# Fourth attention: six multiplications into a free PSUM bank in each unit but a batch's last

## The chip, the cores and the metric

The kernel runs on one core of one Trainium2 chip. The metric is the device time of one execution in microseconds (us): the time before is the median of three runs, 3110.26 us (3109.85 to 3111.97).

## The reference, cut to what matters

The program is a chain of four transformer layers, each an attention-like block and a feed-forward block with a layer norm behind each. The change is in the attention of the fourth layer, for 8 sequences of 256 tokens with 256 channels. What it computes:

```python
q = _rope(x @ Wq)              # 16 heads, two halves of 16 each
k = _rope(x @ Wk)              # 4 key heads, two halves
energy = einsum('bqhad,bkhad->bahqk', q, k)       # a = the two halves
scores = softmax(mask(energy) / sqrt(D))
diff = scores[:, 0] - lam * scores[:, 1]
diff = softmax(mask(diff))
att = einsum('bhqv,bvhd->bqhd', diff, v)
att = att * rsqrt(mean(att * att) + EPS) * rms_w * (1 - LAM_INIT)
return att.reshape(b, s, E) @ Wo
```

So there are two softmaxes with a difference between them, then the product with the values, a norm over each head, and the output projection.

## The kernel before

`l3_attention` (line 1578) is written for five engines that run at the same time and meet only at semaphores. Each engine has its own instruction stream in a fixed order; an instruction waits for a semaphore and everything behind it on that engine waits too.

After the projections, the work goes over batches `b` (one sequence of 256 tokens, two tiles of 128) and, in each batch, over eight **units** `i` from 0 to 7. A unit is one quarter `r = i // 2` of the heads (four heads, one in each group of 32 rows) and one half `a = i % 2` of the head. TensorE's order in a unit is `sequence` (line 1779):

- `scores(b, i)` (line 1708): waits `p_exp`, that is until ScalarE has read the scores of the unit before out of PSUM banks 0 to 3 (there is one set of them), then 16 small multiplications (line 1721) and 8 that add the mask (line 1725); each half signals `s_ps`.
- in odd units `values(b, i)` (lines 1738 to 1752), the product of the turned probabilities with the values, into bank 6 (`OT`); in even units `turn_back` (line 1754), two transposes into bank 7 (`OB`).
- `turn(b, i)` (line 1727): six transposes of the probabilities of the unit three before into banks 4 and 5 (line 1736), when ScalarE has signalled `p_ready`.
- in unit 6 `turn_output` of the batch before (line 1767, into `OT`), in unit 7 `project_output` (line 1775, into `OB`).

VectorE's order in a unit is: `maxima` (line 1961, needs `s_ps`; ScalarE's exponentials need it), in even units half a `difference` (line 1979), `second_maxima` (lines 1989 and 1991), `out_of_psum` (line 1997: it copies what `turn` has put into bank 5), in odd units `values_out` (line 2002) and in even ones `take_output` (lines 2008 and 2009, which signals `on_raw`), and at the end of odd units `ratios` (line 1968 and on, needs `p_exp`) with another half of a `difference`. In unit 5 the norm of the batch before stands between (lines 2016 to 2022), in unit 7 the sum into `x_sb` and its statistics.

ScalarE's order in a unit is: the eight exponentials of the scores with their sums (line 1864), the copy out of bank 4 (line 1872), four exponentials of the second softmax (line 1881, signals `p_ready`). GpSimd adds the mask (line 1816), computes the other half of each difference (lines 1826 and 1829), and squares the output (line 1833).

Batch 0 runs as `opening`, batches 1 to 7 in a loop, and what is left over as `closing`. The waits, the order and the banks are written out by hand; nothing plans them.

Of the kernel before, what the change touches and what calls it, by code (L numbers as in the profile page):

```python
# [30 lines left out]
def bc(ap, axis, n):  # L31

    wide = ap.unsqueeze(axis)
    shape = list(wide.shape)
    shape[axis] = n
    return wide.broadcast_to(tuple(shape))
# [1541 lines left out]
def l3_attention(nc, c, x_sb, mv, xT, w, psum):  # L1578
# [4 lines left out]
    HD, G, R, A = 16, 4, 4, 2  # L1583
# [5 lines left out]
    with ExitStack() as ctx:  # L1589
# [35 lines left out]
        OT, OB = psum[:, 6, :], psum[:, 7, :]  # L1625
# [26 lines left out]
        on_raw = sem("on_raw")  # L1652
# [12 lines left out]
        def live(i, lag, opening, closing):  # L1665

            return i >= lag if opening else i < lag if closing else True
# [5 lines left out]
        with nc.Block() as block:  # L1673
# [14 lines left out]
            def _(pe):  # L1688
                mm = nc.tensor.matmul
# [20 lines left out]
                def scores(b, i, opening):  # L1710
                    r, a = i // A, i % A
                    if i == 0:
                        pe.wait_ge(k_staged, b + 1)
                    if a == 0:
                        pe.wait_ge(q_staged[r], b * 16 + 16)
                    if not (opening and i == 0):
                        pe.wait_ge(p_exp, b * NU + i)
                    for t in range(TT):
                        for g in range(G):
                            rows = slice(32 * g, 32 * g + 32)  # L1720
                            mm(S[:, g, t * P:t * P + (t + 1) * P], qr[rows, a, r, t * P:(t + 1) * P], kr[rows, a, 0:(t + 1) * P],  # L1721
                               start=(t == 0), stop=False, tile_position=(32 * g, 0))
                    for g in range(G):
                        for t in range(TT):
                            last = mm(S[:, g, 2 * t * P:(2 * t + 1) * P], c["idb"], c["maskb"], start=False, stop=(t == TT - 1))  # L1725
                        if g % 2 == 1:
                            last.then_inc(s_ps, 1)

                def turn(b, i):
                    s = b * NU + i - 3  # L1730
                    r, heads = (i - 3) // 2 % R, part(i - 3)
                    pe.wait_ge(p_ready, s + 1)
                    for j, copied in enumerate((pt_even, pt_odd)):
                        pe.wait_ge(copied, s + 1)
                        for k in range(3):
                            last = nc.tensor.transpose(PT[j][:, k * P:(k + 1) * P], pr[:, r, 1, heads.start + j, k * P:(k + 1) * P], c["id"])
                        last.then_inc(pt_ps, 1)

                def values(b, i):
                    q = b * R + (i - 5) // 2  # L1740
                    r = (i - 5) // 2 % R
                    pe.wait_ge(pt_even, 2 * q + 3)
                    pe.wait_ge(pt_odd, 2 * q + 3)
                    if r == 0:
                        pe.wait_ge(v_staged, b * 16 + 16)
                    for g in range(G):
                        cols = slice(32 * g, 32 * g + 32)
                        mm(OT[cols, 0:T], vs[:, 0, g, :], pt[:, r % 2, g, 0:T], start=True, stop=False, tile_position=(0, 32 * g))
                    for g in range(G):
                        cols = slice(32 * g, 32 * g + 32)  # L1750
                        last = mm(OT[cols, P:T], vs[:, 1, g, :], pt[:, r % 2, g, T:T + P], start=False, stop=True, tile_position=(0, 32 * g))
                    last.then_inc(av_ps, 1)

                def turn_back(b, i, first):
                    q = b * R + (i - 6) // 2
                    pe.wait_ge(ots_ready, q + 1)
                    if not first:
                        pe.wait_ge(on_raw, q)
                    for t in range(TT):
                        last = nc.tensor.transpose(OB[:, t * P:(t + 1) * P], ots[:, t * P:(t + 1) * P], c["id"])  # L1760
                    last.then_inc(back_ps, 1)

                def turn_output(b):
                    pe.wait_ge(on_ready, b + 1)
                    for h in range(KD):
                        for t in range(TT):
                            last = nc.tensor.transpose(OT[:, (h * TT + t) * P:(h * TT + t + 1) * P],
                                                       on[:, t, h * P:(h + 1) * P], c["id"])
                    last.then_inc(oT_ps, 1)

                def project_output(b):
                    pe.wait_ge(oT_ready, b + 1)
                    for t in range(TT):
                        for k in range(KD):
                            last = mm(OB[:, t * D:(t + 1) * D], oT[:, k, t * P:(t + 1) * P], wo[:, k, :],
                                      start=(k == 0), stop=(k == KD - 1))
                    last.then_inc(y_ps, 1)

                def sequence(b, opening=False, closing=False):
                    for i in range(NU):  # L1780
                        if not closing:
                            scores(b, i, opening)
                        if i % 2 == 1 and live(i, 5, opening, closing):
                            if i == 7 and not opening:
                                pe.wait_ge(oT_ready, b)
                            values(b, i)
                        if i % 2 == 0 and live(i, 6, opening, closing):
                            if i == 0:
                                pe.wait_ge(z_ready, b)
                            turn_back(b, i, opening)  # L1790
                        if live(i, 3, opening, closing):
                            turn(b, i)
                        if i == 6 and not opening:
                            turn_output(b - 1)
                        if i == 7 and not opening:
                            if not closing:
                                pe.wait_ge(on_raw, b * R + 1)
                            project_output(b - 1)
# [5 lines left out]
                pe.wait_ge(proj_out, NCH * NP)  # L1804
                pe.wait_ge(set_up, 6)
                sequence(0, opening=True)
                with pe.Fori(0, B - 1) as b:
                    sequence(b + 1)
                sequence(B, closing=True)

            @block.gpsimd
# [750 lines left out]
```

## Time and profile before

| | before |
|---|---|
| median of three runs | 3110.26 us |
| the profiled execution's own time | 3111.67 us |
| its span, first to last instruction | 3109.9 us |
| mean granted TensorE clock over the span | 0.917 |
| the fourth attention's units, first scores to last | 2115 to 2573 us |
| one batch in the loop | 58.0 us |

The page gives each engine's busy share of the whole span and, in 40 slices, its busy share and the granted TensorE clock in tenths. The fourth attention lies in slices 28 to 33. The clock has two levels, 1.2 GHz (0.5 in the rows) and 2.4 GHz (1.0); a mean between them over a stretch means that both occurred. Times in the timeline are from the start of the span. A row of the timeline merges instructions of one line that follow each other.

### The profile page before, as it was taken

To read this page: it belongs to the slowest core of one execution; us is meant where nothing else is said; L and a number is where in the kernel's file an instruction comes from. 1 tells how busy PE (TensorE), PEld (TensorE's weight loads), DVE (VectorE), ACT (ScalarE), POOL (GpSimd) and SP (SyncE) were. 2 spreads that over 40 slices of the span, in tenths; PEclk is the share of its full clock that TensorE was granted. 3 is DMA by queue.
4 is the path that set the end of the run, shared out by engine and by line. 5 is a ranking of instruction groups with operands and counts; after the bars stand their busy time and mean duration, and the time that the engine had idled before them with its cause. 6 is when DMAs were issued, how large, how long until landed. Compare 5 with 4: busy or idle time off the path is not lost. (4 is left out here: it accounts for less than half of the span.)

```text
span 3109.9 us, 43072 instructions
## 1 busy us (share of the span) xinstructions
PE 2608.6 (84%) x14256; PEld 1883.3 (61%) x14256; DVE 1858.5 (60%) x4295; ACT 1310.5 (42%) x3605; POOL 359.7 (12%) x392
## 2 busy tenths in 40 slices
PE   7988999889999999998698877796555654999997
PEld 5665544457776777677476665543443433877876
DVE  3665233445464555445645757546888886777777
ACT  4663455533443344334222132205777773332322
POOL 2440000000000000000121000003444440000000
PEclk9998999989999999999899888896777776999998
DMA  3002000000000000002000000100000003000000
GB/s 148 10 7 82 1 0 0 0 35 1 3 3 3 0 3 3 3 0 75 16 0 0 0 0 0 37 6 29 24 19 19 24 9 132 1 1 0 0 0 27
DMA packets 26415, 56.11 MB, mean 18 GB/s; under 512 B 3696, under 2 KB 22896, under 8 KB 24688
## 3 DMA queue, kind: packets, MB, share of 16 engines
q1 hardware_dynamic: 26352, 55.32, 4.8%
q8 instruction: 33, 0.54, 0.1%
q14 instruction: 30, 0.25, 0.0%
HBM read 39.59 MB, written 2.10 MB: 13 GB/s over the span
## 5 line engine op out<-in xcount | busy, mean ns | idle before, releaser
L1864 ACT ACTIVATE l3a_pr<-psum,l3a_nm 128x128 f32<-128x128 f32 (+1 forms) x512 | 207.1, 430 | 202.8 <-DVE l3a_nm L1961 202.8
L1721 PE MATMUL psum<-l3a_kr,l3a_qr 32*128 32x128 f32 (+1 forms) x1024 | 91.1, 491 | 180.3 <-ACT l3a_pr L1864 176.9
L108 DVE TENSOR_TENSOR x_sb<-psum,x_sb 128x512 f32 (+2 forms) x48 | 41.7, 868 | 235.2 <-PE psum L950 135.5
L757 DVE TENSOR_TENSOR l0f_hg<-l0f_sq,psum 128x512 f32<-128x512 f32 x128 | 87.8, 688 | 151.1 <-ACT l0f_sq L689 148.3
L1721 PEld LDWEIGHTS psum<-l3a_kr,l3a_qr 32*128 32x128 f32 x1024 | 51.5, 271 | 198.8 <-ACT l3a_pr L1864 186.3
L995 ACT ACTIVATE l1a_pr<-psum,l1a_nb,l1a_rq 128x128 f32<-128x128 f32 (+1 forms) x256 | 127.2, 509 | 87.2 <-DVE l1a_nb L1048 84.9
L1221 POOL TENSOR_TENSOR l1f_acc<-l1f_t 128x512 f32<-128x512 f32 x4 | 6.3, 1573 | 1334.3 <-DVE l1f_t L1284 1334.3
L2178 PE MATMUL psum<-l3f_x_hi,l3f_w_hi 128*128 x384 | 154.5, 402 | 6.6 <-DVE l3f_w_lo L2261 6.6
L2225 ACT ACTIVATE l3f_sg<-psum 128x512 f32<-128x512 f32 x96 | 57.3, 597 | 240.3 <-PE psum L2181 240.3
L1961 DVE TENSOR_REDUCE l3a_nm<-psum 128x2 f32<-128x256 f32 (+1 forms) x256 | 124.6, 548 | 53.9 <-PE psum L1725 53.9
L2179 PE MATMUL psum<-xT,l3f_w_hi 128*128 x384 | 152.9, 398 | 0.0
L2180 PE MATMUL psum<-l3f_x_hi,l3f_w_lo 128*128 x384 | 152.3, 397 | 0.0
L914 PE MATMUL psum<-l1a_kT,l1a_qT 128*128 128x128 f32 (+1 forms) x512 | 120.2, 359 | 20.9 <-ACT l1a_pr L995 14.0
L2192 PE MATMUL psum<-l3f_w_hi,l3f_h_hi 128*128 128x256 f32 x384 | 127.6, 332 | 7.9 <-DVE l3f_h_lo L2279 7.9
L1816 POOL TENSOR_TENSOR l3a_pr<-l3a_pr,w_l3a_mask 128x1024 f32<-128x1024 f32 x32 | 75.3, 2352 | 486.2 <-ACT l3a_pr L1864 486.2
L652 PE MATMUL psum<-l0f_hg,w_l0f_w 128*128 128x512 f32 x256 | 130.6, 593 | 0.8 <-DVE l0f_hg L757 0.8
L645 PE MATMUL psum<-l0f_xl,w_l0f_w 128*128 x256 | 130.6, 592 | 0.0
L1881 ACT ACTIVATE l3a_pr<-l3a_pr,l3a_nb,l3a_rec 128x128 f32<-128x128 f32 (+1 forms) x256 | 120.8, 581 | 3.8 <-DVE l3a_nb L1991 3.8
L885 PE MATMUL psum<-l1a_xc,w_l1a_q 128*128 128x256 f32 x512 | 122.4, 382 | 0.0
L687 ACT ACTIVATE l0f_relu<-psum 128x512 f32<-128x512 f32 x128 | 76.3, 596 | 108.8 <-PE psum L645 104.4
L867 PE MATMUL psum<-w_l1a_k,l1a_xc 128*128 128x512 f32 x256 | 112.8, 599 | 9.8 <-DMA l1a_xc<-xT 9.8
L891 PE MATMUL psum<-w_l1a_v,l1a_xc 128*128 128x512 f32 x256 | 120.3, 592 | 0.0
(424 smaller groups left out, 6942.2 us busy)
## 6 DMA issues: line engine op xcount, KB each, us to landing
w_l3f_all<-l3f_all_dram SPq DMA_DIRECT2D x1, 9216.0 KB, 25.7
l3a_qr<-l3a_q_all SPq DMA_DIRECT2D x32, 256.0 KB, 2.5
w_l0f_w<-l0f_w_dram SPq DMA_DIRECT2D x2, 2048.0 KB, 10.0
w_l1f_all<-l1f_all_dram SPq DMA_DIRECT2D x1, 2560.0 KB, 8.8
x_sb<-x_dram SPq DMA_DIRECT2D x1, 2048.0 KB, 8.5
l0a_xc<-xT SPq DMA_DIRECT2D x8, 256.0 KB, 2.5
w_l1a_q<-l1a_q_dram SPq DMA_DIRECT2D x1, 2048.0 KB, 7.9
w_l1a_k<-l1a_k_dram SPq DMA_DIRECT2D x1, 2048.0 KB, 13.5
```

Of the source, the lines that this page charges most:

```text
L645: mm(HB[e % 3], w["w1"][:, e, :], xl[:, chunk], start=True, stop=True).then_inc(h_ps, 1)
L652: mm(YL, w["w2"][:, e, :], hg[:, e % 2, :], start=(e == 0), stop=(e == E - 1)).then_inc(used, 1)
L885: last = mm(bank(2 + j % 2)[:, i * T:(i + 1) * T], w["q"][:, k, (2 * j + i) * HD:(2 * j + i + 1) * HD], xc[:, k, :], start=(k == 0), stop= ...
L995: last = nc.scalar.activation(pr[:, n % 2, i, s], S[n % 2][:, i, s], ACT.Exp, bias=nb[:, n % 2, t, i:i + 1], scale=rq[:, t, 2 * n + i:2 * ...
L1721: mm(S[:, g, t * P:t * P + (t + 1) * P], qr[rows, a, r, t * P:(t + 1) * P], kr[rows, a, 0:(t + 1) * P], start=(t == 0), stop=False, tile_p ...
L1864: last = nc.scalar.activation(pr[:, r, a, g, k], S[:, g, k], ACT.Exp, bias=nm[:, i % 2, g, t:t + 1], accum_out=sums[:, r, a, g, t:t + 1])
L1881: last = nc.scalar.activation(pr[:, r, 1, g, k], pr[:, r, 0, g, k], ACT.Exp, bias=nb2[:, r, g, t:t + 1], scale=rec[:, r, 0, g, t:t + 1])
L1961: last = nc.vector.tensor_reduce(nm[:, i % 2, 2 * pair:2 * pair + 2, t], S[:, 2 * pair:2 * pair + 2, t * P:t * P + (t + 1) * P], AX.X, ALU ...
L2178: mm(bk[e % 2], hi, x_hi[:, k, chunk], start=(k == 0), stop=False)
L2179: mm(bk[e % 2], hi, x_lo[:, k, chunk], start=False, stop=False)
L2180: mm(bk[e % 2], lo, x_hi[:, k, chunk], start=False, stop=(k == KD - 1))
L2192: mm(Y[:, t, :], h_hi[:, e % 2, tokens], hi, start=False, stop=False)
```

## The change

A new function `stay_warm(b, i)` is called in each unit of batches 1 to 7, between `values` or `turn_back` and `turn`. In units 0 to 6 it issues six multiplications of a 128x128 bf16 identity (the stationary operand) with the 128x128 bf16 mask read four times over (512 columns), into bank 7 in odd units and bank 6 in even ones. Nothing reads what they write. In units 1, 3 and 5 it waits on `on_raw` first, so that VectorE has read bank 7. In unit 7 it does nothing.

```diff
+                def stay_warm(b, i):
+                    if i in (1, 3, 5):
+                        pe.wait_ge(on_raw, b * R - 2 + i // 2)
+                    if i < 7:
+                        for _ in range(6):
+                            mm(OB if i % 2 else OT, c["idb"], bc(c["maskb"], 1, 4), start=True, stop=True)
+
@@ in sequence(b, opening, closing), for i in range(NU):
                             turn_back(b, i, opening)
+                        if not (opening or closing):
+                            stay_warm(b, i)
                         if live(i, 3, opening, closing):
                             turn(b, i)
```

## Rows read from the trace of the kernel before

**Rows 1.** The page: granted clock in 40 slices.

```profile
PEclk9998999989999999999899888896777776999998
```

**Rows 2.** Windows of one batch long: columns, and the batch that starts at 2457.

```profile
core 0: us, PE busy (x) PEld busy (x) DVE busy (x) ACT busy (x) POOL busy (x), PEclk, DMA share, GB/s
2457.00:2515.00 58.00, 34.30 (x325) 23.10 (x324) 49.45 (x126) 44.00 (x170) 26.75 (x29) 0.76 0.06 20
```

**Rows 3.** Waits of VectorE, batches 1 to 7: total us, times, longest.

```profile
DVE l3a_nm L1961 <- PE psum L1725: 40.3, 32, 2.0
DVE l3a_pt L1997 <- PE psum L1736: 3.4, 11, 0.3
```

**Rows 4.** Timeline, TensorE's scores (start, us, engine, line; idle before): units 0 to 3, 5, 7.

```profile
2457.04 0.94 PE L1721 MATMUL psum<-l3a_kr,l3a_qr 32*128 32x128 f32 x16
2465.73 1.67 PE L1721 MATMUL psum<-l3a_kr,l3a_qr 32*128 32x128 f32 x16 [5.70 <-ACT l3a_pr L1864]
2472.41 0.94 PE L1721 MATMUL psum<-l3a_kr,l3a_qr 32*128 32x128 f32 x16 [1.13 <-ACT l3a_pr L1864]
2478.77 1.66 PE L1721 MATMUL psum<-l3a_kr,l3a_qr 32*128 32x128 f32 x16 [3.37 <-ACT l3a_pr L1864]
2491.80 1.66 PE L1721 MATMUL psum<-l3a_kr,l3a_qr 32*128 32x128 f32 x16 [3.38 <-ACT l3a_pr L1864]
2508.36 1.66 PE L1721 MATMUL psum<-l3a_kr,l3a_qr 32*128 32x128 f32 x16 [5.48 <-ACT l3a_pr L1864]
```

**Rows 5.** Timeline, unit 1: TensorE and VectorE, merged rows.

```profile
2467.97 1.95 DVE L1961 TENSOR_REDUCE l3a_nm<-psum 128x2 f32<-128x256 f32 x4 [1.14 <-PE psum L1725]
2468.30 1.08 PE L1748 MATMUL psum<-l3a_pt,w_l3a_k 128*32 128x256 f32 x8
2469.74 1.54 PE L1736 MATMUL psum<-cf_sb,l3a_pr 128*128 128x128 f32 x6
2471.31 0.56 DVE L1997 COPY l3a_pt<-psum 128x384 f32<-128x384 f32 x1 [0.27 <-PE psum L1736]
2472.39 0.25 DVE L1968 RECIPROCAL l3a_rec<-l3a_sums 128x16 f32<-128x16 f32 x1 [0.19 <-ACT l3a_pr L1864]
2474.35 1.94 DVE L1961 TENSOR_REDUCE l3a_nm<-psum 128x2 f32<-128x256 f32 x4
2474.52 0.87 PE L1736 MATMUL psum<-cf_sb,l3a_pr 128*128 128x128 f32 x6 [0.40 <-ACT l3a_pr L1881]
```

**Rows 6.** Timeline, unit 3, and unit 2's last copy, VectorE's rows.

```profile
2478.75 0.56 DVE L1997 COPY l3a_pt<-psum 128x384 f32<-128x384 f32 x1
2479.46 0.29 DVE L2009 TENSOR_TENSOR w_l3a_q<-psum,l3a_recs 128x128 f32<-128x128 f32 x1
2481.01 1.95 DVE L1961 TENSOR_REDUCE l3a_nm<-psum 128x2 f32<-128x256 f32 x4 [1.26 <-PE psum L1725]
```

**Rows 7.** Timeline, unit 5: VectorE and GpSimd.

```profile
2495.13 2.35 POOL L1816 TENSOR_TENSOR l3a_pr<-l3a_pr,w_l3a_mask 128x1024 f32<-128x1024 f32 x1
2496.95 0.55 DVE L1991 TENSOR_TENSOR l3a_nb<-l3a_nm,l3a_rec 128x4 f32<-128x4 f32 x1
```

**Rows 8.** Timeline, unit 5 of batch 1: TensorE and VectorE.

```profile
2200.68 0.94 PE L1721 MATMUL psum<-l3a_kr,l3a_qr 32*128 32x128 f32 x16 [2.38 <-ACT l3a_pr L1864]
2201.55 1.04 PE L1725 MATMUL psum<-cb_sb 128*128 128x128 bf16 x8
2202.20 1.95 DVE L1961 TENSOR_REDUCE l3a_nm<-psum 128x2 f32<-128x256 f32 x4 [1.28 <-PE psum L1725]
2203.95 1.35 PE L1736 MATMUL psum<-cf_sb,l3a_pr 128*128 128x128 f32 x6
2206.29 0.55 DVE L1997 COPY l3a_pt<-psum 128x384 f32<-128x384 f32 x1
```

**Rows 9.** Window at unit 1's end, columns as in rows 2.

```profile
2471.40:2474.60 3.20, 1.79 (x27) 1.23 (x28) 2.91 (x8) 3.07 (x11) 1.40 (x3) 1.00 0.00 0
```

**Rows 10.** Timeline: the same multiplication in another stage.

```profile
1819.18 0.61 PE L1466 MATMUL psum<-cb_sb 128*128 128x512 bf16 x2
```

## The prediction

> **What bounds the kernel now.** I read the granted clock first: in the fourth attention, slices 28 to 33, it falls to 0.6 to 0.7 [rows 1], and over one batch it is 0.76 while TensorE is busy 34.3 us of 58, VectorE 49.45 and ScalarE 44.00 [rows 2]. So VectorE is nearest to the bound, and TensorE has both idle time and a half clock. The waits say what TensorE still costs: in the loop's seven batches VectorE waited 40.3 us in 32 pieces for the scores before its `maxima`, and 3.4 us for `turn` before its copy [rows 3]. 40.3 is the most that warmer scores could remove, 1.3% of the program.
>
> The timeline shows where. The 16 scores take 0.94 us at 2.4 GHz and 1.66 at 1.2. Those of units 0 and 2 are at the full level, those of 1, 3, 5 and 7 at half, behind idle times of 5.70, 3.37, 3.38 and 5.48 us [rows 4]; the next batch repeats this after 58.0 us. In unit 1 VectorE starts `maxima` 2.24 us after the scores began and waited 1.14 of it; TensorE gets its next scores 4.44 us after `maxima` began [rows 4, 5]. That is a ring: scores, `maxima`, exponentials, next scores. In even units VectorE is the later one: in unit 2 it starts `maxima` 1.94 us after the scores (2472.41 to 2474.35) and waits for nothing, since `ratios` and a `difference` stand ahead. So only odd units have anything to win from a full clock.
>
> **The price of the six multiplications.** I call them dummies. The same form, bf16 with 512 columns, stands in another stage two in a row, 0.61 us together at the full clock [rows 10], of which the last one's way through the array (its tail) is a part. If it is 0.15 of it, each adds 0.23 and six add 1.37 us; that is also the lower bound (without a tail it would be 0.31 each, 1.8). At half clock the mask multiplications of the same kind with a quarter of the columns give 8 in 1.04 us [rows 8]: 0.13 each with the tail, some 0.10 without it, so four times that for 512 columns, 0.41 to 0.52 each. I take 0.41, nearest to the row once its tail is off: 2.47 us for six at half, 3.1 at most. 7 batches x 7 units x 6 are 294 of them. They sit ahead of `turn`, and `turn` has a due time: VectorE's copy (L1997), behind which stand `values_out`, `ratios` and the next `maxima`.
>
> **Even units and unit 6: nothing.** In unit 2 `turn` runs from 2474.52, after 0.40 of waiting, to 2475.39 [rows 5]; VectorE's copy comes at 2478.75 [rows 6]. 1.37 - 0.40 or even 2.47 later is covered by those 3.36 us. In unit 6 `turn_output` moves too, but ScalarE fetches it only behind that unit's exponentials, and unit 7's scores come 5.48 us after TensorE is done. If this cover were gone, each unit would lose at most 2.5 us. What the even units do change is the idle time before the odd scores: 3.37 + 0.40 - 1.37 = 2.4 us before units 3 and 5, and in the same way 4.7 before unit 1; before unit 7 it is 5.48 - 1.37 = 4.1.
>
> **The wait on `on_raw`** (units 1, 3, 5) costs nothing: VectorE's last instruction before it ends at 2479.75 [rows 6], 0.98 us after unit 3's scores begin; at the full clock the scores alone take 0.94, and the masks and `values` stand between them and the dummies.
>
> **Unit 1: +1.2.** Its idle time is still long, so its scores start at half clock as now. Its `turn` still ran at half, 1.54 [rows 5], and from 2471.40 on the clock is full [rows 9]; I put its return at `turn`'s end, 5.55 us after the scores began at 2465.73. Scores and masks take 2.57 us to 2468.30, `values` 1.44 to 2469.74; then 1.5 us of the dummies at half clock, 3.7 of them, the other 2.3 at full, 0.53, and `turn` 0.87: it ends at 2472.7 instead of 2471.28. VectorE wanted it at 2471.04. So the copy is 1.4 later; 0.19 of this was waiting for ScalarE before `ratios` [rows 5], 1.2 is lost. With all dummies and `turn` at full it would end at 4.01 + 1.37 + 0.87 = 6.25 after the scores, 0.5 lost; with all at half at 8.02, 2.3 lost.
>
> **Unit 3: -0.95 or +0.7.** If the clock holds over the new idle time, `maxima` starts 0.95 us sooner: 1.66 - 0.94 = 0.72 from the scores (2.24 to 1.52 in batch 1's row), and for the four masks ahead of it, a half of 1.04, another 0.25. So it starts 1.29 after the scores, not 2.24. Scores with masks and `values` take about half of 2.57 and 1.44, and `turn` then ends at 1.33 + 0.72 + 1.37 + 0.87 = 4.3 us, just when VectorE gets there (1.29 + 3.07 = 4.36; from 2467.97 to 2471.04 in unit 1 it was 3.07). But the nearest row, unit 5 of batch 1 after 2.38 us idle, shows another thing: scores at the full level, 0.94, and the masks behind them at half, 1.04, `maxima` after 1.52, `turn` still partly at half, 1.35 [rows 8]. With that pattern the dummies run mostly at half: masks to 1.8, `values` to 3.25, 2.8 dummies to 4.4 (the clock came back in that `turn`), 3.2 at full to 5.15, `turn` to 6.0, against a due time of 4.6. 1.4 late less 0.72 gained is +0.7. The bounds are -0.95 and, at half throughout, 8.0 against 5.3, +2.6.
>
> **Unit 5: 0 or +0.3.** Here warm scores bring nothing: `nb` (L1991), four numbers a row, took 0.55 us and ended with GpSimd's mask addition, 2497.50 against 2497.48 [rows 7], 5.7 us after the scores (2491.80). In batch 1 `maxima` was 0.72 earlier, and the copy behind still came 5.6 us after the scores [rows 8]. With the clock held `turn` (4.3) is in time; with it falling (6.0) it is 0.3 late; at half throughout 1.3 or more.
>
> **Unit 7: nothing.** It has no dummies, and a 4.1 us idle time before it.
>
> **The sum.** I take the two cases of units 3 and 5 as equally frequent: 1.2 + (-0.95 + 0.7)/2 + 0.3/2 = 1.23 us a batch, 7 batches +8.6 us. Against the profiled execution's own 3111.67 that is 3120.3; against the median, which stood 1.4 lower, 3118.8. No other stage changes.
>
> The rows on the clock over short idle times are mixed: 3.37 us lost it [rows 4], 2.38 us kept it for the scores alone [rows 8]. The Trainium skill ("TensorE: Matmul & The Clock Gate", in "Why this matters for your kernels") has a rule that speaks against my sum: TensorE should have no idle time over some 3 us between bursts, or it falls back to half. By that rule 2.4 us would hold the clock in units 3 and 5 in every batch, and 4.7 and 4.1 would lose it; what that gives is rival 1. On 3.37 the trace agrees with it, on what followed 2.38 it doesn't.
>
> **Rivals.** What a measurement of this kernel can tell from no change is about 0.2%, 6.2 us.
> 1. *The clock holds over 2.4 us in every batch*, and unit 3's gain pays for most of unit 1. 1.2 - 0.95 + 0 = +0.25 a batch, +1.8: 3112. For it: 2.38 us kept the scores full. Against it: it fell right behind them.
> 2. *Faster: the dummies count for more than what they displace.* The clock returns some 1 us sooner in unit 1, so that its `turn` is in time, and holds in unit 3: -0.95 a batch, -6.7: 3103.6. If it held over the long idle times too, units 1, 3 and 7 would gain 0.95 each, 7 x 2.85 = 20: 3090.3. Against it: nothing reaches into unit 1's idle time before its scores, and 5.70 becomes only 4.7.
> 3. *Steeper: the clock is already at half at the scores of units 3 and 5*, as now. Then each of units 1, 3 and 5 has unit 1's case and no gain: 3.6 a batch, +25: 3135. It decides from the point at which 2.4 us of idle time is too long. For it: 3.37 is too long in every batch, and 2.4 is only 1 us shorter. Against it: 2.38 was not too long for the scores [rows 8].
>
> **Chances.** Forecast 0.48 (own range 3113 to 3127; 0.43 of it over +0.2%), rival 1 0.25, rival 2 0.17, rival 3 0.10. So faster 0.17, same 0.30, slower 0.53. The range takes in rival 2's nearer case and most of rival 3: 3101 to 3133. The predicted time is the forecast's, 3118.8.
>
> **What would show it.** Right: VectorE's wait before L1997 for `turn` grows from 3.4 to some 10 to 20 us over the seven batches; its wait before `maxima` falls by 3 to 8 us from 40.3, in unit 3; `turn` in unit 1 ends near 7.0 us after the scores, not 5.55; the batches are 58.5 to 60.5 us apart; the clock of a batch rises from 0.76 to 0.8 or more although the time doesn't fall. Wrong: unit 1's 16 scores take 0.94 (the idle time didn't matter), or the copy's wait stays at 3.4 (the dummies ended in time), or unit 5 gets shorter than 6.68 us from scores to scores.

## The result, and the profile after

| | before | changed |
|---|---|---|
| median | 3111.11 us | 3131.08 us |
| lowest, highest | 3109.85, 3113.69 | 3130.25, 3132.7 |
| ratio, 95% interval | | 1.0064 (1.0046 to 1.0081) |
| profiled execution, span | 3111.67, 3109.9 | 3132.7, 3130.9 |
| clock over the span | 0.917 | 0.924 |

The kernel is 0.64% slower, 20.0 us. The direction is the one forecast, the size is not: 8.6 us were expected. 3131.08 us lies outside the forecast's own range (3113 to 3127) and inside the wide one (3101 to 3133); the nearest single number was rival 3's 3135, which had a chance of 0.10.

The page after, its busy times and its granted clock by slices, has the 294 new multiplications and a faster clock in the fourth attention (slices 28 to 33, against [rows 1]):

```profile
PE 2660.2 (85%) x14550; PEld 1898.0 (61%) x14550; DVE 1861.3 (59%) x4295; ACT 1312.4 (42%) x3605; POOL 359.9 (11%) x392
PEclk9998999999999999999899898896888886999999
```

One batch, the same columns as in [rows 2], is now 61.4 us long. The clock rose from 0.76 to 0.81; VectorE's and ScalarE's work is what it was:

```profile
2408.00:2469.40 61.40, 42.07 (x367) 25.51 (x367) 50.06 (x126) 44.28 (x170) 26.75 (x29) 0.81 0.06 19
```

The waits of VectorE in the loop's batches, the ones of [rows 3]. The one that the change was to shorten fell from 40.3 to 32.9 us; the one for `turn`'s transposes rose from 3.4 to 25.9:

```profile
DVE l3a_nm L1970 <- PE psum L1725: 32.9, 29, 2.0
DVE l3a_pt L2006 <- PE psum L1736: 25.9, 20, 2.0
```

The scores of one batch, as in [rows 4], units 0 to 7 and the next batch's first:

```profile
2408.35 0.94 PE L1721 MATMUL psum<-l3a_kr,l3a_qr 32*128 32x128 f32 x16
2417.14 1.66 PE L1721 MATMUL psum<-l3a_kr,l3a_qr 32*128 32x128 f32 x16 [5.13 <-ACT l3a_pr L1873]
2424.27 0.94 PE L1721 MATMUL psum<-l3a_kr,l3a_qr 32*128 32x128 f32 x16
2431.55 1.67 PE L1721 MATMUL psum<-l3a_kr,l3a_qr 32*128 32x128 f32 x16 [3.62 <-ACT l3a_pr L1873]
2438.31 0.94 PE L1721 MATMUL psum<-l3a_kr,l3a_qr 32*128 32x128 f32 x16
2445.66 0.94 PE L1721 MATMUL psum<-l3a_kr,l3a_qr 32*128 32x128 f32 x16 [3.68 <-ACT l3a_pr L1873]
2451.55 0.94 PE L1721 MATMUL psum<-l3a_kr,l3a_qr 32*128 32x128 f32 x16
2462.62 1.67 PE L1721 MATMUL psum<-l3a_kr,l3a_qr 32*128 32x128 f32 x16 [5.57 <-ACT l3a_pr L1873]
2469.79 0.94 PE L1721 MATMUL psum<-l3a_kr,l3a_qr 32*128 32x128 f32 x16
```

From the start of one unit's scores to the next one's, and against the batch of before that began at 2457.04:

| unit | before | changed | difference |
|---|---|---|---|
| 0 | 8.69 | 8.79 | +0.10 |
| 1 | 6.68 | 7.13 | +0.45 |
| 2 | 6.36 | 7.28 | +0.92 |
| 3 | 6.67 | 6.76 | +0.09 |
| 4 | 6.36 | 7.35 | +0.99 |
| 5 | 6.68 | 5.89 | -0.79 |
| 6 | 9.88 | 11.07 | +1.19 |
| 7 | 6.68 | 7.17 | +0.49 |
| sum | 58.00 | 61.44 | +3.44 |

The first of the seven batches lost nothing: its `project_output` began at 2222.46, before it began at 2222.43. From one `project_output` to the next come 61.22, 61.41, three times 61.4 and 61.51 us against 58.46, 58.25, 57.97 and three times 58.0. By the last batch's `project_output` (2590.91 against 2571.13) 19.8 of the 20.0 us are gone; what is left over behind it took another 0.8.

Unit 1 shows how. TensorE and VectorE, to be read against [rows 5]:

```profile
2419.38 1.95 DVE L1970 TENSOR_REDUCE l3a_nm<-psum 128x2 f32<-128x256 f32 x4 [1.14 <-PE psum L1725]
2419.70 1.08 PE L1748 MATMUL psum<-l3a_pt,w_l3a_k 128*32 128x256 f32 x8
2421.14 2.54 PE L1768 MATMUL psum<-cb_sb 128*128 128x512 bf16 x6
2422.28 0.16 DVE L2000 TENSOR_TENSOR l3a_nb<-l3a_nm,l3a_rec 128x4 f32<-128x4 f32 x1
2423.52 0.82 PE L1736 MATMUL psum<-cf_sb,l3a_pr 128*128 128x128 f32 x6
2424.37 0.56 DVE L2006 COPY l3a_pt<-psum 128x384 f32<-128x384 f32 x1 [1.93 <-PE psum L1736]
```

The six dummies (L1768) run at half clock for 2.54 us, `turn` (L1736) starts 2.4 us behind their start and ends 7.2 us after the scores instead of 5.55, and VectorE, ready at 2422.44, waits 1.93 us for it.

### The profile page after: what moved, and what is told of

The parts are those of the page before. It is cut to its first block and busy times, and to the rows that moved or that the text cites. A ratio compares the mean times of both kernels' runs of the same rounds, so it can differ in the third digit from the quotient of the medians.

```text
span 3130.9 us, 43660 instructions
## 1 busy us (share of the span) xinstructions
PE 2660.2 (85%) x14550; PEld 1898.0 (61%) x14550; DVE 1861.3 (59%) x4295; ACT 1312.4 (42%) x3605; POOL 359.9 (11%) x392
## 5 line engine op out<-in xcount | busy, mean ns | idle before, releaser
L1721 PE MATMUL psum<-l3a_kr,l3a_qr 32*128 32x128 f32 (+1 forms) x1024 | 79.6, 439 | 149.8 <-ACT l3a_pr L1873 146.6
L2234 ACT ACTIVATE l3f_sg<-psum 128x512 f32<-128x512 f32 x96 | 57.3, 597 | 240.5 <-PE psum L2190 240.5
```

## The experiments

"Dummies" are the added multiplications. Theory L: the loss is that `turn` comes late in the odd units, and what follows from it. Theory W: the dummies cost by being there. The kernel before ran beside them again: its medians were 3110.96 us beside e1 to e4, 3110.41 beside e5 to e7 and 3111.48 beside e8 to e10. A time is a median of several executions, a trace is one of them: it can lie some us off the median, and part of that lies outside the fourth attention (its first scores begin between 2112 and 2118 us).

**The same dummies behind `turn`** (e1)

```diff
-                        if not (opening or closing):
-                            stay_warm(b, i)
                         if live(i, 3, opening, closing):
                             turn(b, i)
+                        if not (opening or closing):
+                            stay_warm(b, i)
```

> The same six multiplications (dummies), but issued behind turn instead of ahead of it. Theory L (the loss is that turn, and with it VectorE's copy, comes late in odd units, and that the clock comes back later because of it): the copy's wait falls from 26.2 us back to 3 to 6 us over the stage, batches about 58 us apart instead of 61.43, time 3108 to 3112. Theory W (the dummies cost by being there, wherever they are: work in a half clock, bank or port contention, the queue): at least half of the loss stays, 3120 or more.

Measured: 3106.07 us, ratio 0.9986 (0.9976 to 0.9995): a little faster than before. VectorE's waits in the loop's batches:

```profile
DVE l3a_nm L1970 <- PE psum L1725: 29.3, 29, 1.4
DVE l3a_pt L2006 <- PE psum L1736: 6.1, 9, 2.4
```

The same 294 multiplications, in the other order, cost nothing, and the batches are 57.4 to 58.4 us apart. All of the loss hangs on the place. W falls. The wait for the scores fell further than in the changed kernel, and with `turn` in time 4.9 us of it show.

**Only the odd units** (e2)

```diff
-                    if i < 7:
+                    if i in (1, 3, 5):
                         for _ in range(6):
```

> Dummies only in units 1, 3 and 5, ahead of turn; none in 0, 2, 4, 6. Theory L: the whole loss is here, and it is 1.4 + 1.1 + 0.4 to 1.2 a batch and some 0.5 from the clock's later return in unit 7: 3128 to 3135. Theory W: 18 of the 42 dummies of a batch, so some 40% of the loss, 3119. A third case, that the even units' dummies had to hold the clock and couldn't, gives nothing different from L here.

Measured: 3134.96 us, ratio 1.0073 (1.0056 to 1.009). 18 of 42 dummies a batch make all of the loss; batches are 61.44 us apart. The two waits:

```profile
DVE l3a_nm L1970 <- PE psum L1725: 40.2, 29, 2.0
DVE l3a_pt L2006 <- PE psum L1736: 27.3, 21, 1.8
```

The first stands where it was before the change (40.3). In this kernel unit 5's scores run at half clock too (1.67 us) and its copy comes 0.9 late; units 5 and 6 are 17.55 us together, against 16.96 in the changed kernel, where unit 5 had the full clock. Units 7 and 0 (15.63 against 15.96) and units 1 to 4 (28.26 against 28.52) give this back. That the time is 3.9 us above the changed kernel's doesn't come from the fourth attention: from its first scores to its last `project_output`, leftovers included, it is 501.8 us in this trace and 502.6 in the changed kernel's.

**Only the even units** (e3)

```diff
-                    if i < 7:
+                    if i in (0, 2, 4, 6):
                         for _ in range(6):
```

> Dummies only in units 0, 2, 4 and 6, ahead of turn; none in 1, 3, 5. Here turn is not late (its copy comes 3.4 us later anyway), and the idle time before units 3 and 5 is really 2.4 us, as the prediction had it. Theory L: no loss, batches near 58.0; and if 2.4 us of idle time held the clock at unit 3's scores, up to 0.95 a batch less, 3104; if not, 3111. Theory W: 24 of 42 dummies, 57% of the loss, 3122.

Measured: 3110.72 us, ratio 0.9997 (0.9987 to 1.0007). No loss, as L had it, and no gain. The trace is of an execution of 3118.55 us, 7.8 above the median, so its sums say less: the wait for the scores was 30.5 us (40.3 before), the one for `turn` 7.6 (3.4) and the one for `project_output` 4.4, and the batches were between 57.5 and 60.0 us apart. The idle time before unit 3 was 2.7 us, not 2.4, and it held the clock in some batches and not in others:

```profile
2362.45 0.94 PE L1721 MATMUL psum<-l3a_kr,l3a_qr 32*128 32x128 f32 x16 [2.70 <-ACT l3a_pr L1873]
2419.97 1.67 PE L1721 MATMUL psum<-l3a_kr,l3a_qr 32*128 32x128 f32 x16 [2.69 <-ACT l3a_pr L1873]
```

From one batch's first scores to the next one's, in the loop's batches 2 to 6, it is 57.3 and 57.5 us where unit 3's scores had the full clock, and 58.4, 58.4 and 60.3 where they had not. That a shorter idle time gives back its 0.95 us each time was too simple.

**Unit 1 alone** (e5)

```diff
-                    if i < 7:
+                    if i == 1:
                         for _ in range(6):
```

> Six dummies ahead of turn in unit 1 alone. Theory L: unit 1 and the unit behind it lose what they lost in the changed kernel, 0.45 + 0.92 = 1.4 us a batch, and nothing else changes but the clock's phase in the later units: batches 59 to 59.6 us apart, 3118 to 3122. Rival: each unit's loss hangs on the others through the clock, and one unit's dummies alone are absorbed (batches at 58.0, 3111) or cost the full 3.4 a batch (3131).

Measured: 3118.07 us, ratio 1.0024 (1.0015 to 1.0034): +7.7 us, 1.1 a batch. The batches are 60.3, 58.9, 58.4, 60.2, 58.9 and 60.5 us apart: the mean, 59.5, is the expected one, no single batch is. The 1.1 is not unit 1's term by itself. Units 1 and 2 together are 1.4 us longer than before (13.04) in two batches and at most 0.1 in three, and unit 7, which has no dummies, is 0.4 to 1.2 longer. What unit 1's dummies cost hangs on when the clock comes back. Here they are in two batches, with VectorE's copy behind them:

```profile
2295.99 1.47 PE L1768 MATMUL psum<-cb_sb 128*128 128x512 bf16 x6
2298.16 0.56 DVE L2006 COPY l3a_pt<-psum 128x384 f32<-128x384 f32 x1 [0.66 <-PE psum L1736]
...
2413.05 2.51 PE L1768 MATMUL psum<-cb_sb 128*128 128x512 bf16 x6
2416.26 0.56 DVE L2006 COPY l3a_pt<-psum 128x384 f32<-128x384 f32 x1 [1.90 <-PE psum L1736]
```

At the full clock the copy waits 0.66 us and the two units lose 0.1, at half clock it waits 1.90 and they lose 1.4.

**As many behind `turn` as the idle time holds** (e4)

```diff
-                        for _ in range(6):
+                        for _ in range((20, 2, 10, 2, 10, 2, 20)[i]):
```

> Behind turn, as many dummies as the idle time of each unit holds at the full clock: 20, 2, 10, 2, 10, 2, 20 in units 0 to 6, 0 in 7. Theory L with the clock as the second half of it: the scores of units 1, 3 and 7 go to the full level (0.94 instead of 1.66), each gives back 0.95 us, unit 5 gives nothing since GpSimd's mask ends VectorE's wait there; -2.5 a batch, 3093. If the clock can't be held even so, the 20 dummies at half clock (8.2 us) reach into the next scores: some 3 us a batch slower, 3131. Theory W: the loss grows with the number, 66 against 42, 3142.

Measured: 3110.35 us, ratio 0.9995 (0.9986 to 1.0005). Neither 3093 nor 3131. The clock was held: all scores of the batch below ran in 0.94 us, units 1 to 5 were 5.74 or 6.36 us long, and units 1 and 3 gave back 0.93 each. Unit 7 took more than that, 2.4 us, in this batch. TensorE there, with the next batch's first scores:

```profile
2446.66 0.94 PE L1721 MATMUL psum<-l3a_kr,l3a_qr 32*128 32x128 f32 x16 [3.07 <-ACT l3a_pr L1873]
...
2449.45 1.08 PE L1748 MATMUL psum<-l3a_pt,w_l3a_k 128*32 128x256 f32 x8 [1.30 <-ACT w_l3a_q L1896]
...
2450.89 1.54 PE L1736 MATMUL psum<-cf_sb,l3a_pr 128*128 128x128 f32 x6
2452.22 3.55 PE L1782 MATMUL psum<-l3a_wo,w_l3a_q 128*128 128x256 f32 x8
2455.70 0.94 PE L1721 MATMUL psum<-l3a_kr,l3a_qr 32*128 32x128 f32 x16
```

3.07 us idle before the scores and 1.30 behind them lost the clock in the middle of the unit, where `values`, `turn` and `project_output` follow each other without a pause; 9.04 us instead of 6.68. In other batches the unit took 6.1 to 9.1, 6.11 where the idle time before its scores was 1.68 us. The trace's batches are 55.9 to 58.6 us apart, 57.4 in the mean against 58.1 before; the medians don't show this difference.

**The same with unit 7's idle times filled** (e6)

```diff
-                        for _ in range((20, 2, 10, 2, 10, 2, 20)[i]):
+                        for _ in range((20, 2, 10, 2, 10, 2, 30)[i]):
...
+                            if i == 7 and not (opening or closing):
+                                pe.wait_ge(on_raw, b * R + 1)
+                                for _ in range(5):
+                                    mm(OB, c["idb"], bc(c["maskb"], 1, 4), start=True, stop=True)
                             if i == 7 and not opening:
                                 pe.wait_ge(oT_ready, b)
```

> Dummies behind turn as in e4 (20, 2, 10, 2, 10, 2), with 30 instead of 20 in unit 6 and 5 in unit 7 ahead of values. In e4 all scores ran at the full clock, yet unit 7 gave the gain back: TensorE sat idle 3.07 us before its scores and 1.30 before values, the clock fell, project_output took 3.55 us instead of 1.89, and the next batch began 9.0 us after unit 7's scores instead of 6.7. Theory: with these two idle times filled, project_output stays at 1.89 us and unit 7 at 6 to 6.5; batches near 55.7, time 3093 to 3098. Rival: unit 7 is long for another reason (its values wait for ScalarE's output copy), and it stays at 3108 to 3111.

Measured: 3096.81 us, ratio 0.9952 (0.9935 to 0.9969), batches 55.6 to 56.0 us apart. Units 6 and 7, TensorE:

```profile
2429.67 7.26 PE L1768 MATMUL psum<-cb_sb 128*128 128x512 bf16 x30
...
2437.30 0.94 PE L1721 MATMUL psum<-l3a_kr,l3a_qr 32*128 32x128 f32 x16
...
2438.63 1.24 PE L1794 MATMUL psum<-cb_sb 128*128 128x512 bf16 x5
2439.83 0.64 PE L1748 MATMUL psum<-l3a_pt,w_l3a_k 128*32 128x256 f32 x8
...
2441.32 1.89 PE L1782 MATMUL psum<-l3a_wo,w_l3a_q 128*128 128x256 f32 x8
2443.15 0.94 PE L1721 MATMUL psum<-l3a_kr,l3a_qr 32*128 32x128 f32 x16
```

Unit 7 is 5.85 us long here and 6.1 in most batches. This pair of kernels shows where e4's gain had gone: its idle times in unit 7 lost the clock for the work behind them.

**GpSimd's mask in unit 5 cut short** (e7)

```diff
                 def mask(b, r):
...
+                    if r == 2:
+                        nc.gpsimd.tensor_tensor(pr[:, r, 0, 0, 0:P], pr[:, r, 0, 0, 0:P], w["mask"], ALU.add).then_inc(masked, 1)
+                        return
```

> As e6, but GpSimd's mask addition for the third quarter of the heads (the one that runs in unit 5) is cut from 1024 numbers a row to 128, so that quarter's mask is mostly left out of the output. Theory: in unit 5 VectorE's small operation behind second maxima took 1.18 us instead of 0.16 because it ended with this addition; with the addition short it takes 0.16 to 0.3, and unit 5 with 6 is some 0.9 us shorter: 6 us below e6 over seven batches. Rival: the wait has another cause (the difference before it), and the time is that of e6.

Measured: 3088.64 us, ratio 0.9922 (0.9904 to 0.9939), 8.2 us below the one with the whole mask (6 were expected), batches 54.7 us apart. In the kernel with the whole mask, unit 5, GpSimd and VectorE:

```profile
2423.80 2.35 POOL L1829 TENSOR_TENSOR l3a_pr<-l3a_pr,w_l3a_mask 128x1024 f32<-128x1024 f32 x1
2423.95 1.01 DVE L2002 TENSOR_REDUCE l3a_nm<-l3a_pr 128x2 f32<-128x256 f32 x2 [0.21 <-POOL l3a_pr L1842]
2425.00 1.17 DVE L2004 TENSOR_TENSOR l3a_nb<-l3a_nm,l3a_rec 128x4 f32<-128x4 f32 x1
```

and with the short one:

```profile
2424.76 0.46 POOL L1830 TENSOR_TENSOR l3a_pr<-l3a_pr,w_l3a_mask 128x128 f32<-128x128 f32 x1
2424.91 1.01 DVE L2005 TENSOR_REDUCE l3a_nm<-l3a_pr 128x2 f32<-128x256 f32 x2 [0.20 <-POOL l3a_pr L1845]
2425.95 0.16 DVE L2007 TENSOR_TENSOR l3a_nb<-l3a_nm,l3a_rec 128x4 f32<-128x4 f32 x1
```

VectorE's operation on four numbers a row took 1.17 us because it ended with GpSimd's (2426.17 and 2426.15), and 0.16 without it.

**More dummies in odd units, and batch 0 too** (e8)

```diff
-                        for _ in range((20, 2, 10, 2, 10, 2, 30)[i]):
+                        for _ in range(((16, 16, 16, 12, 12, 6, 10) if opening else (20, 6, 10, 6, 10, 6, 30))[i]):
```

> As e6, with 6 instead of 2 dummies in units 1, 3 and 5, and the idle time of batch 0 filled too (16, 16, 16, 12, 12, 6, 10). In e6 unit 4's scores still ran at half behind 2.23 us of idle time, and batch 0's at half in six of eight units, each with its maxima waiting on them. Theory: unit 4 goes to the full clock (0.3 us a batch, since VectorE is the later one there), batch 0 gets up to 0.95 us in each of about five units: 5 us below e6, 3091. Rival: 6 dummies behind turn in odd units are enough to delay the scores where the clock is at half (6 x 0.41 = 2.5 us): no better than e6 or worse, 3097 to 3105.

Measured: 3091.02 us, ratio 0.9936 (0.992 to 0.9953). The batches in the loop stay at 55.7; the first one's `project_output` begins at 2214.09 instead of 2218.07. So nearly all of the gain is batch 0's. Unit 4's scores had had the full clock in e6 too, but for two batches, and these two were 0.3 us longer than the rest; that is all there was to win. In unit 5 GpSimd's mask still holds VectorE up (L2004 1.18 us).

**The squares later, on GpSimd** (e9)

```diff
+                        if i == 4:
+                            squares(b)
                         difference(b + 1, i)
-                        if i == 2:
-                            squares(b)
```

> As e8, and GpSimd squares the output behind the mask addition of unit 4's scores instead of ahead of the difference two units before, so that this addition ends before VectorE comes to its small operation in unit 5. The output stays whole. Theory (from e7): VectorE's operation takes 0.16 us, unit 5's gain of 0.95 is kept, 6 us below e8, 3085. Rival: the squares, now later, hold up VectorE's norm behind unit 5's copy, and nothing is won.

Measured: 3087.36 us, ratio 0.9924 (0.9907 to 0.994). Batches are 54.43 us apart, 1.27 less, and the clock over one is 1.00. The mask now starts as soon as ScalarE is done and ends before VectorE comes:

```profile
2417.26 2.37 POOL L1829 TENSOR_TENSOR l3a_pr<-l3a_pr,w_l3a_mask 128x1024 f32<-128x1024 f32 x1 [1.39 <-ACT l3a_pr L1877]
...
2421.44 0.16 DVE L2004 TENSOR_TENSOR l3a_nb<-l3a_nm,l3a_rec 128x4 f32<-128x4 f32 x1
```

The whole output is computed. This is the fastest version with the whole output: 24 us less than before, 44 less than changed. Its gain over the one above, 3.7 us by the medians, is smaller than six batches' 7.6; the medians' intervals don't exclude either.

**The squares alone, without dummies** (e10)

The last edit, on the kernel before.

> The kernel before with only GpSimd's squares moved as in e9, no dummies. At half clock in unit 5 VectorE's operation took 0.55 us: theory, it takes 0.16 and the batches are 0.4 us shorter, 3108 (if the clock's phase lets it through). Rival: with cold scores GpSimd is not the later one, no change, 3110.5.

Measured: 3112.14 us, ratio 1.0005 (0.9995 to 1.0014): nothing. The operation does take 0.16 us, and from unit 5's scores to `ratios` it is 9.83 us instead of 10.2; but unit 4's scores now run at half clock and unit 4 is 6.68 us long instead of 6.36. What is won in one unit, the clock takes in another.

## Why the prediction was right in direction and too small

As a whole: the mechanism of unit 1, of the price and of the cover was right, the term of unit 3 was mis-sized and unit 7's was missed. Of the signs named, the clock (0.81) and `turn` in unit 1 (7.2 us) came as said. The wait for `turn` grew to 25.9 us instead of 10 to 20, and the batches were 61.4 us apart instead of 58.5 to 60.5. The wait before `maxima` fell by 7.4 us, within the 3 to 8, but mostly in unit 5, where the scores had the full clock, and not in unit 3. That the time lay in the wide range is in part luck. The range reached that far for rival 3, with 3.6 us a batch in seven batches; 3.44 were lost in six, and they are made up otherwise (unit 5 0.40, units 7 and 0 0.59, where rival 3 had unit 1's case three times).

**The price of the dummies: right.** Six took 1.46 us at the full clock and 2.54 at half, each with its tail; `turn` began 1.29 and 2.38 us behind their start (1.37 and 2.47 were taken).

**Even units' `turn` and the `on_raw` wait: right.** e3 shows no loss from `turn` in them, and in the changed kernel's trace TensorE goes from `values` to the dummies without a wait. What was said of unit 6, covered, holds too.

**Unit 1: right in the changed kernel.** +1.2 was predicted, the sum of units 1 and 2 is +1.37 (0.45 + 0.92; VectorE's `ratios` came later, and this shows in unit 2). `turn` ended at 7.2 us, not 6.95. The size hangs on the point at which the clock comes back: in e5 the same two units lost 1.4 us in two batches and next to nothing in three, less than the 0.5 that the prediction had as its lower bound.

**Unit 3: the step that failed.** "3.37 + 0.40 - 1.37 = 2.4 us before units 3 and 5" kept the even units at 6.36 us. But what unit 1 loses, unit 2 gets longer by: VectorE comes to unit 2's `maxima` 0.92 us later, the exponentials end later, and TensorE, which had done its own work early, waits for them. Its idle time before unit 3 was 3.62 us, longer than before the change. That is 0.92 for unit 2, and 0.3 more because the dummies filled less than worked out: in e3, where unit 2 kept its length, 2.69 us were left. The scores ran at half clock in the six later batches, unit 3 had unit 1's case (and in e3 2.7 us did not hold the clock each time either), and units 3 and 4 lost 0.09 + 0.99 = 1.08 us where -0.12 had been put down. The bounds had this case, and rival 3 (as now, at half in units 3 and 5) named it, for a worse reason. In the first batch, where the scores of units 1 and 3 had the full clock (0.94, behind 1.57 and 2.69 us of idle time), nothing was lost on balance.

**Unit 5: the size right, the condition not.** The idle time before it was 3.68 us, not 2.4, and yet its scores had the full clock, and the masks behind them too (0.62 us); then the clock fell, a little later than in [rows 8]: the dummies took 2.56 us. `turn` ended 6.0 us after the scores, as worked out, and the copy waited 0.32 us for it, as worked out. 0.79 us were won at the next scores and 1.19 lost in unit 6, +0.40 for +0.15 (the mean of 0 and 0.3). That it got shorter than 6.68 us from scores to scores had been named as a sign against the forecast; that sign was ill chosen, since the next scores need the exponentials, and what GpSimd's mask holds up is VectorE's copy, which shows one unit later. The mask as the holder-up, read from one row of [rows 7], is shown by e7 and e9.

**Unit 7: "nothing" was wrong.** It lost 0.49, with unit 0 0.59. It has no dummies, but its clock came back later within the unit (`turn` 1.28 us instead of 0.87), `project_output` started 5.34 instead of 4.77 us after the scores, and the next batch's scores stand right behind it. e4 shows the same at its worst, e6 shows it mended. Why the clock comes back later there isn't settled: the idle time before the scores is nearly the same (5.57 us instead of 5.48), the moment at which the unit starts isn't, nor is what TensorE did in unit 6. Unit 6's dummies aren't needed for it: in e5, which has none there, unit 7 is 7.1 to 7.9 us long. Nor did they shorten the idle time before unit 7 to the 4.1 us worked out: `turn_output` stands behind them and waits for VectorE's norm in any case, so they only filled part of that wait. It is in unit 6 of the changed kernel:

```profile
2456.39 0.66 PE L1774 MATMUL psum<-cf_sb,w_l3a_q 128*128 128x128 f32 x4 [1.17 <-DVE w_l3a_q L2031]
```

In the batch's terms: 1.37 + 1.08 + 0.40 + 0.59 = 3.44 us for 1.23, in six batches instead of seven: 20.6 for 8.6.

**Rival 1 and the rule beside it fall, in an instructive way.** The idle time that should have been 2.4 us was 3.6 to 3.7 in both units. By the Trainium skill ("TensorE: Matmul & The Clock Gate", in "Why this matters for your kernels"), both are over some 3 us and should have lost the clock. The trace agrees for unit 3 (3.62) and not for unit 5 (3.68, with scores in 0.94 us). In e1 2.07 us kept the full clock in one batch and lost it in the next. The idle time alone doesn't say which.

**What is left open.** That the place of the dummies makes the loss is shown by e1 to e3. That the phase between the work and the clock decides where the full clock is kept is argued from the pairs of batches, not shown by a run that moves the phase alone. Nor was a version tried in which an odd unit's dummies are fewer ahead of `turn`.

## What to carry to other kernels

Fill an engine's idle time behind the instruction that another engine is next to wait for; ahead of it only where that instruction is not due yet, as in the even units (e3). Ask of each piece of idle time what stands ahead of it in the queue and when that is due; the same six multiplications cost 20 us ahead of the transposes and gave 5 back behind them. A busier clock is no sign of a faster kernel: here it rose from 0.76 to 0.81 in a batch that got 3.4 us longer, and the batch got 2.3 us shorter when its idle times were filled to the end, and 3.6 with GpSimd's order changed as well. When one unit gets longer, work out the next one's idle time anew.

## What the runs showed of the hardware that had not been expected

- The same idle time of TensorE before the same instruction gave either clock: in the changed kernel 3.61 to 3.69 us before unit 3 half and 3.68 or 3.69 before unit 5 full in each of six batches, 3.69 before unit 5 half in the first, 2.07 us before unit 3 full and half in two batches of e1, 2.23 us full in units 2 and 6 of e6 and half in unit 4 of the same batch. The work ahead of these idle times ran at the full clock. Where it was lost, it fell within the idle time. The changed kernel's windows before unit 3 and before unit 5, each from some 2 us into the idle time to just before the scores (columns as in [rows 2]):

```profile
2430.00:2431.50 1.50, 0.00 (x0) 0.00 (x0) 1.47 (x4) 1.50 (x9) 0.17 (x1) 0.56 0.00 0
2444.00:2445.60 1.60, 0.00 (x0) 0.00 (x0) 1.53 (x5) 1.60 (x9) 0.00 (x0) 1.00 0.00 0
```

- In e6 a VectorE operation on four numbers a row stretched from 0.16 to 1.17 us to end with a GpSimd operation on other data that had begun 1.2 us before it; the reductions just before it, while the same GpSimd operation ran, took their usual 1.0 for two. So not all of VectorE's operations are held up: this one, which multiplies two SBUF operands, was. By the Trainium skill ("SBUF — State Buffer", "SBUF: two separate sides") VectorE and GpSimd share a pair of ports that one instruction holds whole, and a VectorE operation with two SBUF inputs needs it beside a GpSimd operation that reads SBUF; the trace agrees (1.17 us against 0.16).
- In some kernels the batches settle at one length, in others they don't: 57.97 to 58.01 us in the last four before, 61.41 to 61.51 in the last five of the changed kernel, 54.42 or 54.43 in e9; but 57.4, 57.7, 58.3, 57.8, 58.4 and 57.7 in e1, and 55.9 to 58.6 in e4. The program does the same work in each of them.
